# Another order of the sixteen scratch steps of a batch, and other chunks for the value halves

## The chip, the cores and the metric

The kernel runs on one NeuronCore of one Trainium2 chip. The metric is the time of one execution on the device in microseconds (us); smaller is better. TensorE (PE, with PEld for its weight loads) multiplies, ScalarE (ACT) and VectorE (DVE) read its results from PSUM, GpSimd (POOL) and SyncE (SP) do small work and start transfers.

## The reference

One block of cross attention and a mixture of experts, all in float32: 32 batches of 100 tokens of width 128, each batch with its own context of 1444 rows, 16 heads of width 8.

```python
q, k, v = LN(x) @ W_q.T, ctx @ W_k.T, ctx @ W_v.T         # 16 heads of 8
scores  = einsum('bhqd,bhkd->bhqk', q, k) / sqrt(8)
e       = exp(clip(scores, -50, 50)); attn = e / sum(e)
x = x + einsum('bhqk,bhkd->bhqd', attn, v) @ W_o.T
z = LN(x)
comb = top-2 softmax weights of z @ gate_w                # 8 experts
x = x + sum_e comb[e] * (gelu(z @ w1[e]) @ w2[e])
```

## The kernel before

Most of the time goes to the attention, a loop over the 32 batches `b` (function `attend`, once for each engine; the batches 0, 1, 30 and 31 are written out, the others are a hardware loop over pairs). The 1444 keys are 12 tiles of 128 and the 16 heads are 4 groups of 4, so a batch has 48 pairs of a tile and a group; three pairs make a **chunk**, and a batch has 16 chunks, c = 0 to 15. The three matmuls of a chunk (L689) fill one of two PSUM buffers, `scores`. ACT takes the exponential of the chunk (L902) into a ring of 8 chunks in SBUF, `probs`, and DVE clips it there (L1046).

The product with the values has a tile and a half of the heads as its unit, a **half** `h` = 0 to 23. Its four matmuls (L701) each use 17 of the array's columns, one in each of the four column groups, and add to `o_sum`. A matmul in float32 leaves two records, so a half is 8 records, and a row x24 is three halves. `HALF_AT[h]` (L70) is the chunk at which PE does half h; a number of 16 or more means chunk HALF_AT[h] - 16 of the next batch. Half h needs the clipped chunk `LAST_CHUNK[h // 2]`. Chunk c may overwrite its place in the ring once the halves that read chunk c - 8 are done (L901).

Everything else of a batch goes through one further PSUM bank, `scratch`: 16 **scratch steps**, one in each chunk, in the order of the list `STEPS` (L109).

- For the next batch, `PREPARE`: turn 0 to 2 transpose the context (L614) and ACT copies it to `ctxT` (L862); key 0 to 2 project a third of the keys each (L619, 512 columns, the last 420), ACT copies to `k_full` (L866), and DVE splits it in a high and a low part (L960, L962) one chunk later; value 0 to 2 project a third of the values (L630) and DVE copies to `v_both` (L984); query (L624).
- For the batch before, `FINISH`: heads transposes its sums (L662) after DVE took them from `o_sum` (`take_sums`, L1051); queries, project, tokens; gate gives the logits of the experts, with which DVE finds the two best; rank (L682, L683) counts places in the experts' lists.

Since there is one bank, every scratch step waits until the step ahead of it has been copied out: `pe.wait_ge(scratch_emptied, step)` at L645. In a chunk PE does, in this order: the scores of chunk c + 1 (after the exponential of chunk c - 1), the scratch step of chunk c, the halves of chunk c. ACT does the exponential of chunk c, then the copy of the scratch step, if it is ACT's. DVE clips chunk c - 1, then takes its scratch step. The chunks of `take_sums` (L1153), of `pick` (L1167) and of ACT's `second_share` (L906) follow from `HALF_AT` and `STEPS` through `HALF_AT[-1]` and `GATED`. In batch 0 the places of `FINISH` are filled by transposes of normed tokens (L638), and batch 31 has only the steps of `FINISH`. After the attention come the experts, 57 tiles of 128 rows (L797 to L818), which the change leaves alone.

Of the kernel before, what the change touches and what calls it, by code (L numbers as in the profile page):

```python
# [48 lines left out]
def xattn_moe(nc, x, ctx, mask, W_q, W_k, W_v, W_o, gate_w, w1, w2, out):  # L49
# [15 lines left out]
    RING = 8  # L65
    LAST_CHUNK = [(t * GROUPS + GROUPS - 1) // CB for t in range(TILES)]
    HALVES = 2 * TILES
    LAG = 2

    HALF_AT = [4 * (h // 6) + LAG + (2, 2, 2, 4, 4, 4)[h % 6] for h in range(HALVES)]  # L70
    KC = 4
    KSTEPS = TILES // KC

# [27 lines left out]
    PREPARE = [("query", 0)]  # L101
# [4 lines left out]

    FINISH = [("heads", 0), ("queries", 0), ("project", 0), ("tokens", 0), ("gate", 0), ("rank", 0)]

    STEPS = (PREPARE[1:7] + FINISH[:3] + PREPARE[:1] + PREPARE[7:8] + FINISH[3:5] + PREPARE[8:] + FINISH[5:])  # L109
    IN_LAST = [s in FINISH for s in STEPS]  # L110

    ALONE = PREPARE[7:9] + [("first query", n) for n in range(2)] + PREPARE[9:]

    FIRST_STEPS = [s if s in PREPARE else ("norm", QSTEPS - len(FINISH) + FINISH.index(s)) for s in STEPS]
    assert len(STEPS) == CHUNKS and QSTEPS - len(FINISH) == 2
    PROJECTED, GATED = STEPS.index(("project", 0)), STEPS.index(("gate", 0))

    def scratch_step(b, c):

        if isinstance(b, int) and b == B - 1:  # L120
            c = sum(IN_LAST[:c])
        return len(STEPS) * b + len(ALONE) + c

    def planned(b, c):
# [3 lines left out]
        if isinstance(b, int) and b == B - 1 and not IN_LAST[c]:  # L128
            return None, 0
        return STEPS[c]  # L130

# [4 lines left out]
    def later(b, least=1):  # L136

        return not isinstance(b, int) or b >= least
# [7 lines left out]
    with es:  # L146
# [463 lines left out]
        def _(pe):  # L610
# [84 lines left out]
            def weigh_values(p, h):  # L695


                t, s = divmod(h, 2)
                for g in range(GROUPS):
                    c, m = divmod(t * GROUPS + g, CB)  # L700
                    last = nc.tensor.matmul(o_sum[32 * g:32 * g + VW, s * PQ:(s + 1) * PQ],  # L701
                                            v_ones[p][:, t, 2 * g + s, :],
                                            probs[:, c % RING, m, s * PQ:(s + 1) * PQ],
                                            start=(t == 0 and s == 0), stop=(t == TILES - 1),
                                            skip_group_check=True)
                last.then_inc(pv_done, 1)
# [32 lines left out]
            def attend(i, p, b, last_one):  # L739
                for c in range(CHUNKS):  # L740
# [20 lines left out]
                    for h in range(HALVES):  # L761
                        if HALF_AT[h] == c:
                            pe.wait_ge(probs_ready, CHUNKS * b + LAST_CHUNK[h // 2] + 1)
# [5 lines left out]
                            weigh_values(p, h)  # L769
                        elif HALF_AT[h] == c + CHUNKS and later(b):  # L770
                            pe.wait_ge(probs_ready, CHUNKS * (b - 1) + LAST_CHUNK[h // 2] + 1)
# [9 lines left out]
            for h in range(HALVES):  # L781
                if HALF_AT[h] >= CHUNKS:
                    pe.wait_ge(probs_ready, CHUNKS * (B - 1) + LAST_CHUNK[h // 2] + 1)
# [168 lines left out]
        def _(dve):  # L952
# [95 lines left out]
            def take_sums(b):  # L1048

                dve.wait_ge(pv_done, HALVES * (b + 1))  # L1050
                nc.vector.tensor_copy(o_raw[:], o_sum[:, 0:GQ]).then_inc(o_taken, 1)  # L1051
# [99 lines left out]
            def attend(p, b):  # L1151
                for c in range(CHUNKS):
                    if c == HALF_AT[-1] + 1 - CHUNKS and later(b):  # L1153
                        take_sums(b - 1)
# [143 lines left out]
```

## Time and profile before

| what | us |
|---|---|
| median of 3 runs | 1141.67 (1141.52 to 1142.09) |
| the profiled execution | 1142.76 |
| its span, first to last instruction | 1140.8 |
| PE busy | 1042.8 (91%) |
| DVE busy | 757.6 (66%) |
| ACT busy | 741.4 (65%) |
| POOL busy | 258.4 (23%) |

Between 100 and 850 us the granted clock of TensorE is 1.00, that is 2.4 GHz. "Idle before" in a row of the trace is the time that the engine had nothing running before that group, with what released it. Matmuls overlap their neighbours, and their ends are modelled, so the distance between the starts of two rows tells more than their durations.

### The profile page before, as it was taken

The page shows a single profiled execution, that of the slowest core. Times are in us where ns is not written, and L with a number is a line of the kernel's source. Part 1 is how long each engine was busy: PE and PEld are TensorE (multiplying, and loading weights), DVE is VectorE, ACT ScalarE, POOL GpSimd, SP SyncE. Part 2 cuts the span into 40 slices and gives each one's busy share as a digit, 9 for nine tenths or more (in the row PEclk, how much of TensorE's full clock was granted, in tenths as well). Part 3 has the DMA queues.
Part 4 walks back from the last instruction along what each step waited for, and adds up shares of the span by engine and source line. Part 5 has one row for each costly group of instructions (what it writes and reads, how often), then busy time and mean ns, then how long its engine had stood idle before and what let it go on. Part 6 is the DMA issues. An engine that isn't in the chain of part 4 may idle for free.

```text
span 1140.8 us, 30886 instructions
## 1 busy us (share of the span) xinstructions
PE 1042.8 (91%) x10544; PEld 761.5 (67%) x10545; DVE 757.6 (66%) x1956; ACT 741.4 (65%) x960; POOL 258.4 (23%) x324
## 2 busy tenths in 40 slices
PE   4699999999999999999999999999999999399990
PEld 3466666666666666666666666666666667299990
DVE  4557777777777777777777777777777777434443
ACT  2477777777777777777777777777777777244440
POOL 3711111111111111111111111111111112145554
PEclk8699999999999999999999999999999999699995
DMA  6644454444444444445445454444545545022216
GB/s 195 194 151 160 161 170 164 156 158 161 165 164 161 165 156 162 164 169 167 166 166 169 169 169 166 167 167 169 169 169 169 169 140 156 15 68 64 63 48 173
DMA packets 144306, 172.68 MB, mean 151 GB/s; under 512 B 32225, under 2 KB 88549, under 8 KB 144277
## 3 DMA queue, kind: packets, MB, share of 16 engines
q1 hardware_dynamic: 139380, 165.67, 44.0%
q0 software_dynamic: 4896, 6.63, 2.1%
q8 instruction: 17, 0.28, 0.1%
q14 instruction: 13, 0.10, 0.0%
HBM read 36.83 MB, written 22.08 MB: 52 GB/s over the span
## 4 chain that ended last, share of the span: by engine, by line
PE 85%; ACT 3%; DVE 3%; DMA 2%; SPq 2%; issue 2%; POOL 0%; ACTq 0%; POOLq 0%; DVEq 0%
PE o_sum L701 26%; PE scores L689 25%; PE scratch L630 8%; PE scratch L619 7%; PE scratch L614 5%; PE scores L807 5%; PE scores L818 4%; ACT k_full L866 3%; DVE v_both L984 2%; PE scratch L662 2%; DMA x_all<-in_x_dram 1%; SPq L486 1%; PE scratch L667 1%; SPq L405 1%; PE scores L797 1%
## 5 line engine op out<-in xcount | busy, mean ns | idle before, releaser
L902 ACT ACTIVATE probs<-scores 128x1200 f32<-128x1200 f32 x512 | 589.3, 1180 | 88.9 <-PE scores L689 85.9
L689 PE MATMUL scores<-q_stack,k_stack 128*128 128x400 f32 x1536 | 431.5, 395 | 10.4 <-DVE mask_f L1033 10.0
L1046 DVE TENSOR_SCALAR probs<-probs 128x1200 f32<-128x1200 f32 x512 | 387.0, 782 | 49.1 <-ACT probs L902 47.7
L689 PEld LDWEIGHTS scores<-q_stack,k_stack 128*128 128x128 f32 x1536 | 256.0, 190 | 138.6 <-issue 99.0
L701 PE MATMUL o_sum<-probs,v_both 128*17 128x200 f32 x6144 | 309.8, 334 | 0.1
L701 PEld LDWEIGHTS o_sum<-probs,v_both 128*17 128x17 f32 x6144 | 154.8, 97 | 84.1 <-issue 16.7
L573 POOL DMA_INDIRECT expert_rows<-rows,row_atu x64 | 77.5, 1211 | 373.8 <-DMA expert_rows<-fill 314.9
L630 PE MATMUL scratch<-w_turned,ctxT 128*128 128x128 f32 x768 | 108.3, 284 | 8.5 <-DVE v_both L984 7.2
L866 ACT COPY k_full<-scratch 128x512 f32<-128x512 f32 (+1 forms) x93 | 52.2, 561 | 92.9 <-PE scratch L619 91.7
L630 PEld LDWEIGHTS scratch<-w_turned,ctxT 128*128 128x128 f32 x768 | 96.1, 192 | 24.3 <-DVE v_both L984 17.6
L563 POOL TENSOR_SCALAR rstd<-moments 100x1 f32<-100x1 f32 x32 | 37.7, 1177 | 289.5 <-DVE moments L1084 289.5
L619 PE MATMUL scratch<-ctxT,w_turned 128*128 128x512 f32 x186 | 91.0, 571 | 0.0
L984 DVE COPY v_both<-scratch 128x512 f32<-128x512 f32 x93 | 64.1, 689 | 37.8 <-PE scratch L630 35.7
L960 DVE CAST k_hi<-k_full 128x512 fp32r<-128x512 f32 (+1 forms) x93 | 38.7, 416 | 58.4 <-ACT k_full L866 33.4
L597 POOL DMA_INDIRECT expert_outputs<-ctx_nat,tile_home x57 | 57.2, 1004 | 64.6 <-DVE ctx_nat L1248 60.7
L962 DVE TENSOR_TENSOR k_lo<-k_full,k_hi 128x512 fp32r<-128x512 f32 (+1 forms) x93 | 61.5, 661 | 3.2
L818 PE MATMUL scores<-w_sb,k_full 128*128 x456 | 61.6, 279 | 1.3 <-ACT k_full L933 1.3
L807 PE MATMUL scores<-ctxT 128*128 128x128 f32 x456 | 62.4, 281 | 0.0
L933 ACT ACTIVATE k_full<-scores 128x512 f32<-128x512 f32 x57 | 34.1, 598 | 40.2 <-PE scores L807 39.6
L818 PEld LDWEIGHTS scores<-w_sb,k_full 128*128 128x128 f32 x456 | 56.3, 194 | 1.7 <-issue 1.5
L807 PEld LDWEIGHTS scores<-ctxT 128*128 128x128 f32 x456 | 57.1, 197 | 0.3
L862 ACT COPY ctxT<-scratch 128x512 f32<-128x512 f32 (+1 forms) x93 | 52.5, 565 | 4.1 <-PE scratch L614 0.9
(142 smaller groups left out, 753.0 us busy)
## 6 DMA issues: line engine op xcount, KB each, us to landing
k_stack<-k_hi SPq DMA_DIRECT2D x192, 256.0 KB, 2.5
k_stack<-k_lo SPq DMA_DIRECT2D x192, 256.0 KB, 2.6
expert_rows<-fill SPq DMA_DIRECT2D x32, 406.2 KB
xT_and_ctx<-in_ctx_dram SPq DMA_DIRECT2D x16, 704.0 KB
ctx_nat<-in_ctx_dram SPq DMA_DIRECT2D x16, 704.0 KB
q_rep<-q_parts SPq DMA_DIRECT2D x128, 50.0 KB, 1.9
q_stack<-q_rep SPq DMA_DIRECT2D x128, 50.0 KB, 1.9
v_both<-expert_rows SPq DMA_DIRECT2D x57, 65.0 KB, 1.8
```

What stands on the lines that cost most here:

```text
L573: nc.gpsimd.indirect_dma_start(out=expert_rows[0:E * CAP, :], out_offset=bass.IndirectOffsetOnAxis(ap=row_atu[:, k:k + 1], axis=0), in_=ro ...
L619: return nc.tensor.matmul(into[:, 0:KEYS[k]], w_turned[:, WK, :], ctxT[:, KEY_COLS[k]], start=True, stop=True)
L630: last = nc.tensor.matmul(scratch[:, j * P:(j + 1) * P], ctxT[:, t * P:(t + 1) * P], w_turned[:, WV, :], start=True, stop=True)
L689: last = nc.tensor.matmul(scores[:, c % 2, m, 0:GQ], k_stack[p][:, g, t * P:(t + 1) * P], q_stack[p][:, :, g, :], start=True, stop=True)
L701: last = nc.tensor.matmul(o_sum[32 * g:32 * g + VW, s * PQ:(s + 1) * PQ], v_ones[p][:, t, 2 * g + s, :], probs[:, c % RING, m, s * PQ:(s + ...
L807: last = nc.tensor.matmul(scores[:, n % 2, 0, c * P:(c + 1) * P], w1_tile[:, n % 2, c * P:(c + 1) * P], tileT[:, n % 2, :], start=True, st ...
L818: last = nc.tensor.matmul(scores[:, n % 2, 1, 0:D], hiddenT[:, n % 2, c, :], w2_sb[:, bass.ds(expert, 1), c, :].rearrange("f o d -> f (o d)"),
L866: nc.scalar.copy(k_full[:, k, 0:KEYS[k]], scratch[:, 0:KEYS[k]]).then_inc(scratch_emptied, 1)
L902: nc.scalar.activation(probs[:, c % RING, :, :], scores[:, c % 2, :, 0:GQ], ACT.Exp, scale=SCALE).then_inc(exp_ready, 1)
L962: nc.vector.tensor_tensor(k_lo[:, cols], k_full[:, k, 0:KEYS[k]], k_hi[:, cols].bitcast(F32), ALU.subtract).then_inc(k_split, 1)
L984: nc.vector.tensor_copy(v_ones[p][:, k * KC:(k + 1) * KC, :, 0:2 * DH], scratch[:].rearrange("p (t n d) -> p t n d", t=KC, n=PAIRS)).then_ ...
L1046: nc.vector.tensor_scalar(chunk, chunk, LOW, HIGH, ALU.max, ALU.min).then_inc(probs_ready, 1)
```

## The change

It writes out two tables. `STEPS` has the three turns and the three keys as turn, turn, key, turn, key, key (before: turn, key three times), and at the end value 2, gate, value 1, rank (before: gate, value 1, value 2, rank). `HALF_AT` spreads the halves of the chunks 0 to 6: before, the chunks 0, 2, 4 and 6 had three halves each and the odd chunks none; now the chunks 0 to 6 have 1, 1, 2, 1, 1, 1 and 4. Chunk 14 has four instead of three. The last half of a batch moves from chunk 2 of the next batch to chunk 3, and with it `take_sums` from chunk 3 to chunk 4; gate moves from chunk 12 to 13, `pick` from 13 to 14 and `second_share` from 14 to 15. No instruction of arithmetic is added or removed. All line numbers after L108 grow by one.

```diff
-    LAG = 2
-    HALF_AT = [4 * (h // 6) + LAG + (2, 2, 2, 4, 4, 4)[h % 6] for h in range(HALVES)]
+    HALF_AT = [4, 5, 6, 6, 6, 6, 8, 8, 8, 10, 10, 10, 12, 12, 12, 14, 14, 14, 14, 16, 17, 18, 18, 19]
...
-    STEPS = (PREPARE[1:7] + FINISH[:3] + PREPARE[:1] + PREPARE[7:8] + FINISH[3:5] + PREPARE[8:] + FINISH[5:])
+    STEPS = [("turn", 0), ("turn", 1), ("key", 0), ("turn", 2), ("key", 1), ("key", 2),
+             ("heads", 0), ("queries", 0), ("project", 0), ("query", 0), ("value", 0), ("tokens", 0),
+             ("value", 2), ("gate", 0), ("value", 1), ("rank", 0)]
```

PE in the loop's even batches, chunks 2 to 5, before. L614 are turns, L619 keys, L701 halves (x4 is one half), L689 the scores of a chunk:

```order
L614 MATMUL scratch<-ident,ctx_nat1 128x128 x4
L701 MATMUL o_sum<-probs,v_both 17x200 x4
L771 REGISTER_ALU
L701 MATMUL o_sum<-probs,v_both 17x200 x8
L744 REGISTER_ALU
L689 MATMUL scores<-q_stack0,k_stack0 128x400 x3
L645 REGISTER_ALU
L619 MATMUL scratch<-ctxT,w_turned 128x512
L744 REGISTER_ALU
L747 ISA
L689 MATMUL scores<-q_stack0,k_stack0 128x400 x3
L645 REGISTER_ALU
```

The same engine after, from key 0 in chunk 2 to the scores of chunk 4:

```order
L620 MATMUL scratch<-ctxT,w_turned 128x512
L702 MATMUL o_sum<-probs,v_both 17x200 x4
L772 REGISTER_ALU
L702 MATMUL o_sum<-probs,v_both 17x200 x4
L745 REGISTER_ALU
L690 MATMUL scores<-q_stack0,k_stack0 128x400 x3
L646 REGISTER_ALU
L615 MATMUL scratch<-ident,ctx_nat1 128x128 x3
L615 MATMUL scratch<-ident,ctx_nat1 128x36
L702 MATMUL o_sum<-probs,v_both 17x200 x4
L745 REGISTER_ALU
L748 ISA
```

Before, a key had only scores between it and the next step; after, every turn and every key has halves right behind it.

PE in the chunks 12 to 14 before (L675 gate, L630 value):

```order
L675 MATMUL scratch<-gate_sb,zT 100x8
L701 MATMUL o_sum<-probs,v_both 17x200 x12
L689 MATMUL scores<-q_stack0,k_stack0 128x400 x3
L645 REGISTER_ALU
L630 MATMUL scratch<-w_turned,ctxT 128x128 x4
L689 MATMUL scores<-q_stack0,k_stack0 128x400 x3
L645 REGISTER_ALU
L630 MATMUL scratch<-w_turned,ctxT 128x128 x4
L701 MATMUL o_sum<-probs,v_both 17x200 x12
```

And after:

```order
L631 MATMUL scratch<-w_turned,ctxT 128x128 x4
L702 MATMUL o_sum<-probs,v_both 17x200 x12
L690 MATMUL scores<-q_stack0,k_stack0 128x400 x3
L646 REGISTER_ALU
L676 MATMUL scratch<-gate_sb,zT 100x8
L690 MATMUL scores<-q_stack0,k_stack0 128x400 x3
L646 REGISTER_ALU
L631 MATMUL scratch<-w_turned,ctxT 128x128 x4
L702 MATMUL o_sum<-probs,v_both 17x200 x16
```

The gate now stands between the two value steps, and each value step has halves behind it.

## Rows read from the trace of the kernel before

**Rows 1.** The page: span, busy time by engine, and the group of the halves.

```profile
span 1140.8 us, 30886 instructions
...
PE 1042.8 (91%) x10544; PEld 761.5 (67%) x10545; DVE 757.6 (66%) x1956; ACT 741.4 (65%) x960; POOL 258.4 (23%) x324
...
L701 PE MATMUL o_sum<-probs,v_both 128*17 128x200 f32 x6144 | 309.8, 334 | 0.1
```

**Rows 2.** Timeline, PE: value 2 of batch 1 and of batch 30.

```profile
98.85 1.16 PE L630 MATMUL scratch<-w_turned,ctxT 128*128 128x128 f32 x8 [0.23 <-DVE v_both L984]
...
949.61 1.16 PE L630 MATMUL scratch<-w_turned,ctxT 128*128 128x128 f32 x8 [0.23 <-DVE v_both L984]
```

**Rows 3.** Waits of PE, 100 to 900 us: total us, times, longest us.

```profile
PE scratch L630 <- DVE v_both L984: 6.2, 27, 0.2
PE scratch L614 <- ACT k_full L866: 6.0, 29, 0.2
PE scratch L614 <- issue: 5.6, 26, 0.3
```

**Rows 4.** Timeline, PE, chunks 0 to 6 of one batch: start us, us, what.

```profile
513.50 0.60 PE L614 MATMUL scratch<-ident,ctx_nat 128*128 128x128 f32 x4
514.03 1.21 PE L701 MATMUL o_sum<-probs,v_both 128*17 128x200 f32 x24
...
515.83 1.02 PE L619 MATMUL scratch<-ctxT,w_turned 128*128 128x512 f32 x2
...
517.63 0.65 PE L614 MATMUL scratch<-ident,ctx_nat 128*128 128x128 f32 x4 [0.24 <-issue]
...
520.01 1.02 PE L619 MATMUL scratch<-ctxT,w_turned 128*128 128x512 f32 x2
...
521.78 0.73 PE L614 MATMUL scratch<-ident,ctx_nat 128*128 128x128 f32 x4 [0.21 <-ACT k_full L866]
...
524.24 0.87 PE L619 MATMUL scratch<-ctxT,w_turned 128*128 128x420 f32 x2
...
525.77 0.64 PE L662 MATMUL scratch<-ident,o_raw 128*100 128x128 f32 x4
```

**Rows 5.** Timeline, PE, chunks 10 to 14 of the same batch.

```profile
531.06 0.80 PE L689 MATMUL scores<-q_stack,k_stack 128*128 128x400 f32 x3
531.70 1.15 PE L630 MATMUL scratch<-w_turned,ctxT 128*128 128x128 f32 x8
532.77 1.21 PE L701 MATMUL o_sum<-probs,v_both 128*17 128x200 f32 x24
...
534.57 0.25 PE L671 MATMUL scratch<-ident,rows 100*128 100x100 f32 x1
...
535.23 0.27 PE L675 MATMUL scratch<-gate_sb,zT 128*100 128x8 f32 x2
...
537.23 1.05 PE L630 MATMUL scratch<-w_turned,ctxT 128*128 128x128 f32 x8
538.03 0.79 PE L689 MATMUL scores<-q_stack,k_stack 128*128 128x400 f32 x3
539.06 1.16 PE L630 MATMUL scratch<-w_turned,ctxT 128*128 128x128 f32 x8 [0.23 <-DVE v_both L984]
```

**Rows 6.** Timeline, ACT in chunks 1 and 2, DVE in chunk 13 of the same batch.

```profile
516.99 0.59 ACT L866 COPY k_full<-scratch 128x512 f32<-128x512 f32 x1 [1.19 <-PE scratch L619]
517.47 1.18 ACT L902 ACTIVATE probs<-scores 128x1200 f32<-128x1200 f32 x1
518.54 0.59 ACT L862 COPY ctxT<-scratch 128x512 f32<-128x512 f32 x1
...
538.31 0.69 DVE L984 COPY v_both<-scratch 128x512 f32<-128x512 f32 x1 [1.08 <-PE scratch L630]
```

**Rows 7.** Timeline, PE in batch 31: halves, with two chunks of scores between.

```profile
953.53 1.21 PE L701 MATMUL o_sum<-probs,v_both 128*17 128x200 f32 x24
...
955.97 1.21 PE L701 MATMUL o_sum<-probs,v_both 128*17 128x200 f32 x24
```

## Prediction

> **What bounds the kernel now.** I read the page first: PE is busy 91% of the span, DVE and ACT two thirds [rows 1]. Then the timeline of PE over many batches: it repeats itself, and from value 2 of batch 1 to value 2 of batch 30 it takes 949.61 - 98.85 = 850.76 us, 29.34 us for each of the 29 batches [rows 2]. So whatever the change does, it does some thirty times. Then the waits of PE: only three kinds, each about once a batch or less, and the longest is 0.3 us [rows 3]. Their sum over 27 batches is 17.8 us, which makes them look small: 0.66 us a batch. The timeline of one batch shows that they cost more than their idle time says, and where.
>
> I read that timeline from the start of one scratch step to the start of the next, a "block", because the starts don't depend on modelled ends. Blocks with halves behind the step have room for the copy: turn 0 to key 0 takes 515.83 - 513.50 = 2.33 us, turn 1 to key 1 2.38, turn 2 to key 2 2.46 [rows 4]. Blocks with only scores are too short for it: key 0 to turn 1 takes 1.80, key 1 to turn 2 1.77, key 2 to heads 1.53, value 1 to value 2 1.83 [rows 4, 5]. For a value step the part that isn't waiting can be read: the scores start 538.03 - 537.23 = 0.80 us after it, and with no wait the next step starts 0.64 us after the scores (531.06 to 531.70). That is 1.44 us, so this wait costs 1.83 - 1.44 = 0.39 us, not the 0.23 of its row [rows 5]. What it waits for is DVE's copy, which starts 538.31 - 537.23 = 1.08 us after the value step and takes 0.69 [rows 6]. The key steps wait in the same way for ACT's copy, 516.99 - 515.83 = 1.16 us after the step, and 0.59 long [rows 4, 6].
>
> **What halves cost.** The change takes the waits away by putting halves behind each of those steps. The halves aren't new, but a group of them has a fixed part. In a row x24 the four column groups work at once, so it is six rounds of four records; one record takes 0.334 us, and the last round starts 1.21 - 0.334 = 0.88 us after the first, 0.175 us a round [rows 1, 5]. A half is two rounds, 0.35 us. From the start of a group of three halves to the next scratch step are 534.57 - 532.77 = 1.80 us [rows 5]; so with one half it is 1.10, with two 1.45, with four 2.15. Of the 1.80, 1.05 are the six rounds and about 0.6 the scores; the rest, 0.1 to 0.15, and a gap between the scratch step and the group, is what each group adds. Before there are 8 groups a batch, after there are 11.
>
> The distance from a scratch step to the group behind it is 514.03 - 513.50 = 0.53 for a turn and 532.77 - 531.70 = 1.07 for a value step [rows 4, 5]. For a **key** step the trace never shows it, since no key has halves behind it. This is the one number that I must bound. Both groups above start 0.07 to 0.08 us before the modelled end of the step (0.60 and 1.15); by that a key of 512 columns gives 1.02 - 0.07 = 0.95 [rows 4, 5]. The latest is when ACT can read the result, 1.16 [rows 6]. I take 0.98, close to the low end, since for turn and value the group starts so near the modelled end; and 0.15 less, 0.83, for the key of 420 columns, whose row is 0.15 shorter [rows 4].
>
> **Chunks 0 to 6, block by block, after.** Turn 0 with one half to turn 1: 2.33 less two halves, 1.63. Turn 1 to key 0: 1.63. Key 0 with two halves to turn 2: 0.98 + 1.45 = 2.43. Turn 2 with one half to key 1: 2.46 - 0.70 = 1.76. Key 1 to key 2: 0.98 + 1.10 = 2.08. Key 2 to heads: 0.83 + 1.10 = 1.93. Sum 11.46 us; before it was 525.77 - 513.50 = 12.27 [rows 4]. Heads has one half more behind it, + 0.35. Together - 0.46 us a batch.
>
> **Chunks 11 to 14.** Before: tokens to gate 0.66, gate to value 1 2.00, value 1 to value 2 1.83, value 2 with three halves 2.87 as value 0 shows: 7.36 [rows 5]. After: tokens to value 2 0.66 (it waits for the same copy as gate did), value 2 with three halves 2.87, gate with only scores to value 1, value 1 with four halves 3.22. The gate block isn't in the trace: its low end is 0.66, the block of tokens, whose row is as short (0.25 against 0.27), its high end the 1.44 of a value step without a wait; I take 0.75, by the likeness of the rows. Sum 7.50, + 0.14 us a batch.
>
> **Do other waits come?** After turn 0, ACT has 1.10 us from the start of the halves to turn 1, and needs some 0.1 + 0.59 for its copy. ACT itself has an exponential and a copy in every chunk: 0.48 us from a copy to the exponential behind it (516.99 to 517.47) and 1.07 from that to the next copy (518.54), 1.55 in all [rows 6]. The two shortest blocks are 1.63, so ACT just keeps up for two chunks, and the next, 2.43, gives it air. What covers it is thin, 0.08 us a block; if it were gone, turn 1 would start late by the 0.1 or so that is missing, and by the same again at key 0. DVE's move of its copy of `o_sum` by a chunk puts the split of key 0 ahead of it; half 0 waits for that copy, and it has the scores and key 1 in between, about 0.64 + 0.98 us, against a copy of 400 columns, shorter than the 0.69 us of 512 [rows 5, 6]. The gate moves behind a clip on DVE, and picking the two best experts now comes one chunk later, with four halves ahead of rank to hide it. ACT's small exponential of the gate stands behind that of chunk 15 now, and DVE's part of rank waits for it; ACT has no copies in the chunks 12 to 14, so it is ahead there. SP's and POOL's queues keep their order; key 0 is split one chunk later, and its transfers are wanted only in chunk 15. I cost all of these at nothing.
>
> **The sum.** - 0.46 + 0.14 = - 0.32 us a batch, thirty batches: - 9.6 us. Batch 0 loses the wait between its value steps (- 0.39) and does one half more (+ 0.35): nothing. Batch 31 has the three groups more without the waits: a group of three halves with two chunks of scores takes 955.97 - 953.53 = 2.44, less 1.05 for the rounds and 2 x 0.6 for the scores leaves 0.2 a group, + 0.6 us [rows 7]. The half fewer after the last chunk I credit at nothing, since that stretch ends with the last clip. Total - 9.0 us. Against the profiled execution, 1142.8 (its span of 1140.8 [rows 1] and 2.0 around it), that is 1133.8; the median of the runs lies 1.1 lower, 1141.67, so **1132.7 us**, 0.8% faster.
>
> **The rivals.** *Better*: the group starts behind a key as soon as its columns have passed. The low end is the 0.10 us that a turn has above its four matmuls; the keys then save another 0.1 each, and the restarts after a wait go too (turn 1 to key 1 is 0.05 longer than turn 0 to key 0, turn 2 to key 2 0.13 [rows 4]): 0.3 to 0.45 us a batch more, 1119 to 1124 us.
>
> *No change*: the waits go, but ACT or DVE gives some back, 0.1 at each of turn 1, key 0 and value 1. Then - 0.32 becomes 0: 1141 to 1143 us. For it speaks the thin cover of ACT in the chunks 0 and 1; against it, that each engine has a third of its time free [rows 1].
>
> *Slower*: the array can't go over from a wide matmul to the halves before the wide one has wholly left it. A key then gives 1.16 us to its group instead of 0.98 [rows 4, 6], + 0.18 for three keys, + 0.54 a batch: - 0.32 becomes + 0.22, 30 x 0.22 = 6.6, 1148 us. It decides from 1.09 us for a key: 0.98 + 0.32 / 3. For it speaks that there are three groups more in every batch whatever happens to the waits; against it, that turn and value show the group starting before their modelled ends [rows 4, 5]. The Trainium skill, TensorEngine Tiling (Array Packing), section Key Properties, has a rule that speaks against this change: going from one tiling mode to another drains TensorE. The trace agrees in kind: 1.07 us from a value step to its halves, 0.80 from one to its scores [rows 5]. The page has no price for it, so by the page alone the three groups more would be a loss of unknown size.
>
> **Chances.** The forecast, 1128 to 1138: 0.56. Better: 0.14. No change and its neighbourhood up to 1144: 0.18. Slower beyond: 0.12. For the range, 1124 to 1145 leaves about 0.1 on each side. A measurement of this kernel can tell some 0.2%, 2.3 us, from no change; faster than 1139.4 gets 0.76, between that and 1144.0 gets 0.12, slower 0.12.
>
> **What would show it.** In the trace of after: no idle time of PE before L615, L631 and L663 in the loop (right), or a new row of waits on ACT before L615 (the second rival). A distance from L620 of 512 columns to the L702 behind it of about 0.98; 1.09 or more gives the third rival. The block of one half after a turn 1.63, the gate block 0.75. The period of a batch 29.0 us. The prediction is wrong if the groups cost more in a mix of short ones than in threes, which no row of before shows.

## Result and profile after

The changed kernel takes 1127.31 us in the median of 4 runs (1125.29 to 1128.25), against 1141.88 (1141.52 to 1143.66) before: ratio 0.9863, 95% interval 0.9849 to 0.9878, or 14.6 us less. The profiled execution took 1127.23 us.

The page of after answers to [rows 1]: the span, the busy times, the group of the halves.

```profile
span 1125.1 us, 30886 instructions
...
PE 1047.4 (93%) x10544; PEld 752.2 (67%) x10545; DVE 761.0 (68%) x1956; ACT 744.2 (66%) x960; POOL 274.7 (24%) x324
...
L702 PE MATMUL o_sum<-probs,v_both 128*17 128x200 f32 x6144 | 328.1, 335 | 0.5 <-DVE probs L1047 0.5
```

The three kinds of waits of [rows 3] have no successor: between 100 and 900 us the list of PE's waits is empty. PE's busy time grew by 4.6 us while the span fell by 15.7: what the waits gave back was in part spent on more and smaller groups of halves. They are busy 328.1 us where they were 309.8, with no half added: a row of one half lasts 0.53 us, a row of three 1.21 and not 3 x 0.53, so splitting a group adds about 0.2 us to the busy time. The starts of the rank step in batch 1 and in batch 30 give the period of a batch, (935.88 - 101.56) / 29 = 28.77 us, where it was 29.34 [rows 2].

```profile
101.56 0.27 PE L683 MATMUL scratch<-chosen,before 100*100 100x8 f32 x2
...
935.88 0.26 PE L683 MATMUL scratch<-chosen,before 100*100 100x8 f32 x2
...
957.54 0.31 PE L683 MATMUL scratch<-chosen,before 100*100 100x8 f32 x2
```

The same steps in the kernel before: rank of the batches 1, 30 and 31.

```profile
101.73 0.26 PE L682 MATMUL scratch<-chosen,before 100*100 100x8 f32 x2
...
952.50 0.26 PE L682 MATMUL scratch<-chosen,before 100*100 100x8 f32 x2
...
973.09 0.34 PE L682 MATMUL scratch<-chosen,before 100*100 100x8 f32 x2
```

These six rows hold the whole account of the two spans. Up to the rank step of batch 1 after is 0.17 us earlier; the next 29 batches take 834.32 instead of 850.77 us, 16.45 less; batch 31 takes 957.54 - 935.88 = 21.66 instead of 20.59, 1.07 more; what follows takes 0.15 less (1125.1 - 957.54 = 167.56 against 1140.8 - 973.09 = 167.71). Sum: - 15.7 us.

Timeline of PE after, chunks 0 to 6 of one batch, answering to [rows 4] (L615 turns, L620 keys, L702 halves, L663 heads):

```profile
505.30 0.60 PE L615 MATMUL scratch<-ident,ctx_nat 128*128 128x128 f32 x4
505.83 0.53 PE L702 MATMUL o_sum<-probs,v_both 128*17 128x200 f32 x8
...
506.95 0.60 PE L615 MATMUL scratch<-ident,ctx_nat 128*128 128x128 f32 x4
...
508.60 1.02 PE L620 MATMUL scratch<-ctxT,w_turned 128*128 128x512 f32 x2
509.55 0.87 PE L702 MATMUL o_sum<-probs,v_both 128*17 128x200 f32 x16
510.36 0.82 PE L690 MATMUL scores<-q_stack,k_stack 128*128 128x400 f32 x3
511.02 0.67 PE L615 MATMUL scratch<-ident,ctx_nat 128*128 128x128 f32 x4
...
512.73 1.02 PE L620 MATMUL scratch<-ctxT,w_turned 128*128 128x512 f32 x2
...
514.80 0.87 PE L620 MATMUL scratch<-ctxT,w_turned 128*128 128x420 f32 x2
...
516.73 0.60 PE L663 MATMUL scratch<-ident,o_raw 128*100 128x128 f32 x4
...
519.39 0.25 PE L666 MATMUL scratch<-ident,attn 100*128 100x100 f32 x1
```

No row has an idle time. The halves start 509.55 - 508.60 = 0.95 us after the key. From turn 0 to heads are 11.43 us, and heads takes 2.66 to the next step. The chunks 11 to 15, answering to [rows 5] (L672 tokens, L631 values, L676 gate, L683 rank):

```profile
525.81 0.25 PE L672 MATMUL scratch<-ident,rows 100*128 100x100 f32 x1
...
526.47 1.09 PE L631 MATMUL scratch<-w_turned,ctxT 128*128 128x128 f32 x8
527.48 1.21 PE L702 MATMUL o_sum<-probs,v_both 128*17 128x200 f32 x24
...
529.27 0.26 PE L676 MATMUL scratch<-gate_sb,zT 128*100 128x8 f32 x2
...
530.02 1.05 PE L631 MATMUL scratch<-w_turned,ctxT 128*128 128x128 f32 x8
531.01 1.55 PE L702 MATMUL o_sum<-probs,v_both 128*17 128x200 f32 x32
...
533.14 0.26 PE L683 MATMUL scratch<-chosen,before 100*100 100x8 f32 x2
```

Value 2 with three halves takes 2.80 to the next step, the gate 0.75, value 1 with four halves 3.12.

### The profile page after: what moved, and what is told of

The parts are those of the page before. It is cut to its first block, busy times and chain, and to the rows that moved or that the text cites. A ratio compares the mean times of both kernels' runs of the same rounds, so it can differ in the third digit from the quotient of the medians.

```text
span 1125.1 us, 30886 instructions
## 1 busy us (share of the span) xinstructions
PE 1047.4 (93%) x10544; PEld 752.2 (67%) x10545; DVE 761.0 (68%) x1956; ACT 744.2 (66%) x960; POOL 274.7 (24%) x324
## 4 chain that ended last, share of the span: by engine, by line
PE 91%; DMA 3%; SPq 2%; DVE 2%; issue 1%; ACT 0%; POOL 0%; POOLq 0%; DVEq 0%
PE scores L690 32%; PE o_sum L702 27%; PE scratch L631 8%; PE scratch L620 7%; PE scores L808 5%; PE scores L819 4%; PE scratch L615 4%; DMA x_all<-in_x_dram 1%; SPq L487 1%; PE scratch L663 1%; PE scratch L668 1%; SPq L406 1%; PE scores L798 1%; PE scratch L625 1%; PE scratch L684 1%
## 5 line engine op out<-in xcount | busy, mean ns | idle before, releaser
L690 PE MATMUL scores<-q_stack,k_stack 128*128 128x400 f32 x1536 | 406.3, 380 | 10.4 <-DVE mask_f L1034 9.9
L690 PEld LDWEIGHTS scores<-q_stack,k_stack 128*128 128x128 f32 x1536 | 248.6, 189 | 129.3 <-issue 73.3
L702 PE MATMUL o_sum<-probs,v_both 128*17 128x200 f32 x6144 | 328.1, 335 | 0.5 <-DVE probs L1047 0.5
L702 PEld LDWEIGHTS o_sum<-probs,v_both 128*17 128x17 f32 x6144 | 145.0, 97 | 144.2 <-issue 58.0
L631 PE MATMUL scratch<-w_turned,ctxT 128*128 128x128 f32 x768 | 106.2, 282 | 1.3 <-ACT v_both L892 0.7
L631 PEld LDWEIGHTS scratch<-w_turned,ctxT 128*128 128x128 f32 x768 | 96.1, 192 | 10.2 <-ACT q_full L874 4.7
L620 PE MATMUL scratch<-ctxT,w_turned 128*128 128x512 f32 x186 | 90.2, 566 | 0.0
```

The costliest lines, as they stand in the source:

```text
L620: return nc.tensor.matmul(into[:, 0:KEYS[k]], w_turned[:, WK, :], ctxT[:, KEY_COLS[k]], start=True, stop=True)
L631: last = nc.tensor.matmul(scratch[:, j * P:(j + 1) * P], ctxT[:, t * P:(t + 1) * P], w_turned[:, WV, :], start=True, stop=True)
L690: last = nc.tensor.matmul(scores[:, c % 2, m, 0:GQ], k_stack[p][:, g, t * P:(t + 1) * P], q_stack[p][:, :, g, :], start=True, stop=True)
```

## Experiments

Two theories were set against each other. **Prices**: each wait behind a long copy has its price, and each group of halves has one; the change swaps the one for the other, and the sum of the blocks tells the time. **Evenness**: the gain comes from chunks of more even length. All kernels below do the whole computation.

| kernel | ratio to before | 95% interval | period of a batch, us |
|---|---|---|---|
| before | 1 | | 29.34 |
| changed | 0.9863 | 0.9849 to 0.9878 | 28.77 |
| values' order alone | 0.9897 | 0.9880 to 0.9915 | 28.97 |
| halves alone | 0.9960 | 0.9946 to 0.9974 | 29.15 |
| all steps, halves of before | 0.9916 | 0.9900 to 0.9933 | 29.06 |
| changed, three groups more | 1.0047 | 1.0028 to 1.0066 | 29.47 |
| changed, beside the next three | 0.9865 | 0.9848 to 0.9881 | 28.77 |
| changed, turns 0 and 2 bare | 0.9870 | 0.9854 to 0.9887 | 28.77 |
| new order, ten groups | 0.9932 | 0.9915 to 0.9948 | 28.93 |
| new order, project covered | 0.9917 | 0.9901 to 0.9934 | 28.91 |

Each ratio is to the kernel before, run beside that kernel on the same chip. The periods are read as above, rank of batch 1 to rank of batch 30, divided by 29. They have far less spread than the times: the two profiles of the changed kernel have spans of 1125.1 and 1121.7 us and the same period.

**The values' order alone.**

```diff
-             ("heads", 0), ..., ("tokens", 0), ("gate", 0), ("value", 1), ("value", 2), ("rank", 0)]
+             ("heads", 0), ..., ("tokens", 0), ("value", 2), ("gate", 0), ("value", 1), ("rank", 0)]
```

> Only the last four scratch steps are new (value 2, gate, value 1, rank); turns, keys and the halves are as before. Price theory: a wait behind a value step costs 0.39 us, and the four blocks from tokens to rank go from 7.37 us to about 7.0 with the halves of before, so 0.37 us a batch, 11 us in all, ratio to before 0.990. The waits of PE on ACT's copies of the keys stay, 0.2 to 0.3 us each. Rival, evenness theory (the gain comes from chunks of more even length, not from single waits): nothing or under 3 us, since the chunks are as uneven as before.

Measured 0.9897 and 0.37 us a batch less, as the prices had it; evenness, with under 3 us, fell. The waits of PE on the copies of the keys are still there (first the list of PE's waits, of which this is the largest, then the timeline of PE, key 0 and turn 1):

```profile
PE scratch L615 <- ACT k_full L867: 6.5, 31, 0.3
...
509.12 1.02 PE L620 MATMUL scratch<-ctxT,w_turned 128*128 128x512 f32 x2
509.58 1.11 PE L690 MATMUL scores<-q_stack,k_stack 128*128 128x400 f32 x3
510.91 0.66 PE L615 MATMUL scratch<-ident,ctx_nat 128*128 128x128 f32 x4 [0.22 <-issue]
```

So two thirds of the gain, 0.37 of 0.57 us, come from putting the gate between two value steps, in a stretch where no group of halves was added.

**The halves alone.**

```diff
-    HALF_AT = [4 * (h // 6) + LAG + (2, 2, 2, 4, 4, 4)[h % 6] for h in range(HALVES)]
+    HALF_AT = [4, 5, 6, 6, 6, 6, 8, 8, 8, 10, 10, 10, 12, 12, 12, 14, 14, 14, 14, 16, 17, 18, 18, 19]
```

> Only the halves are spread as in the change; the order of the scratch steps is the old one. Price theory: the waits behind the keys go, three groups of halves at 0.28 us each come, the wait between the two value steps stays: 0.23 us a batch less than before, 7 us, ratio 0.994. Rival, evenness theory: most of the 15 us of the change, ratio near 0.988.

Measured 0.9960 and 0.19 us a batch less; evenness, with 0.988, fell here too. The waits behind the keys are gone, and the one between the value steps is the only one left in the list of PE's waits:

```profile
PE scratch L631 <- DVE v_both L985: 6.3, 27, 0.2
```

0.37 and 0.19 add up to 0.56; the whole change has 0.57. What is left for the third part of the change, the order of turns and keys, is 0.01. No kernel leaves out that part alone, but the timeline of this one confirms it. From turn 0 to heads, with the old order and the halves spread, are 522.60 - 511.18 = 11.42 us, and 11.43 in the changed kernel:

```profile
511.18 0.60 PE L615 MATMUL scratch<-ident,ctx_nat 128*128 128x128 f32 x4
...
522.60 0.60 PE L663 MATMUL scratch<-ident,o_raw 128*100 128x128 f32 x4
```

With the halves spread, that order is worth nothing.

**All steps, halves of before.** The new `STEPS` with the old `HALF_AT`.

> Only the order of the scratch steps is new; the halves are where they were, in eight groups of three. Bare of halves are now turn 1, turn 2 and key 2. Price theory: a turn without halves is followed by the next step after about 1.25 us (copy seen 0.6 after its start, 0.59 long) where 1.04 is the least, so it costs 0.2 to 0.25, less than the 0.28 of a group; sum of the blocks from turn 0 to rank 21.2 us against 22.0 before and 21.4 in the changed kernel: 24 us less than before, 7 less than the changed kernel, ratio 0.979. Rival, evenness theory: slower than the changed kernel, 0.99 at best, since its chunks are as uneven as before.

Measured 0.9916, 29.06 us. It is slower than the changed kernel, and by 0.09 us a batch slower than with the values' order alone; 24 us less than before had been expected, 9.0 were measured. Two reasons stand in the timeline, PE first, for turn 1 and key 0 in a batch of even and one of odd number:

```profile
512.17 0.60 PE L615 MATMUL scratch<-ident,ctx_nat 128*128 128x128 f32 x4
512.52 0.79 PE L690 MATMUL scores<-q_stack,k_stack 128*128 128x400 f32 x3
513.89 1.13 PE L620 MATMUL scratch<-ctxT,w_turned 128*128 128x512 f32 x2 [0.57 <-issue]
...
541.45 0.60 PE L615 MATMUL scratch<-ident,xT_and_ctx 128*128 128x128 f32 x4
...
542.72 1.13 PE L620 MATMUL scratch<-ctxT,w_turned 128*128 128x512 f32 x2
```

ACT in the same two places:

```profile
513.25 0.59 ACT L863 COPY ctxT<-scratch 128x512 f32<-128x512 f32 x1 [1.11 <-PE scratch L615]
...
542.09 0.59 ACT L863 COPY ctxT<-scratch 128x512 f32<-128x512 f32 x1 [0.66 <-PE scratch L615]
```

In the odd batch a turn without halves takes 1.27 us to the next step, as expected. In the even one it takes 1.72, since ACT starts its copy 1.08 us after the turn instead of 0.64, though it had nothing else to do. The list of PE's waits has this 13 times:

```profile
PE scratch L620 <- issue: 6.9, 12, 0.6
PE scratch L620 <- ACT ctxT L863: 1.3, 1, 1.3
```

The timeline says where: in batch 4, the longest (1.33 us idle), and in the batches 6, 8, to 28 (0.53 to 0.60). These are the 13 passes of the loop's body that follow a jump back. In batch 2, the first pass of the same code, the same turn takes 1.27 us (105.00 to 106.27), and so it does in batch 30, which is written out (919.13 to 920.40). So the delay goes with the jump back and not with the code. The changed kernel doesn't show it: there the exponential on ACT runs up to this copy, which starts 0.64 us after turn 1 in an even batch too. And a key behind a turn without halves needs 0.10 us more (a row of 1.13 instead of 1.02) before its halves start, which the expectation had left out.

Evenness had this kernel right, but it had the two before wrong.

**Three groups more.**

```diff
-    HALF_AT = [4, 5, 6, 6, 6, 6, 8, 8, 8, 10, 10, 10, 12, 12, 12, 14, 14, 14, 14, 16, 17, 18, 18, 19]
+    HALF_AT = [4, 5, 6, 6, 6, 6, 8, 8, 9, 10, 10, 11, 12, 12, 13, 14, 14, 14, 14, 16, 17, 18, 18, 19]
```

> The changed kernel with one half of each of the chunks 8, 10 and 12 moved to the chunk behind it (9, 11 and 13), where no copy is late: three groups of halves more, no wait taken away. Price theory: 3 x 0.28 = 0.84 us a batch more than the changed kernel, 25 us, so ratio to before about 1.008. Rival (a group costs next to nothing, what the change bought was the waits): equal to the changed kernel, 0.986.

Measured 1.0047, 0.70 us a batch more than the changed kernel: 0.23 us for each group, not 0. With no wait in sight, moving three halves by one chunk makes the kernel slower than the one before. Block by block, the group behind the query costs 0.31, the one behind tokens 0.31 and the one behind the gate 0.22, 0.28 in the mean as expected. The sum is smaller because the first of them bought something. Timeline of PE, query to tokens:

```profile
503.54 0.36 PE L625 MATMUL scratch<-xT_and_ctx,w_turned 128*128 x2
503.83 0.53 PE L702 MATMUL o_sum<-probs,v_both 128*17 128x200 f32 x8
...
504.95 1.05 PE L631 MATMUL scratch<-w_turned,ctxT 128*128 128x128 f32 x8
505.93 0.87 PE L702 MATMUL o_sum<-probs,v_both 128*17 128x200 f32 x16
```

Value 0 reaches its halves after 0.98 us here, and after 1.07 in the kernel before [rows 5]. Before, it stood right behind the query with only scores between, and its first weight load waited for ACT's copy of the query. That is in the list of all waits of the kernel before (100 to 900 us), and not in the list of this one:

```profile
PEld scratch L630 <- ACT q_full L873: 4.5, 27, 0.2
```

It is a wait of the weight load, which PE's own list does not have, because the scores were still running. The change leaves it: the changed kernel has it 28 times, 4.7 us in all.

**Turns bare.** From the changed kernel; nine groups. To make room in the chunks 4 and 5, chunk 6 has two halves instead of four, and the last half of a batch is back in chunk 2.

```diff
+    HALF_AT = [4, 4, 5, 5, 6, 6, 8, 8, 8, 10, 10, 10, 12, 12, 12, 14, 14, 14, 14, 17, 17, 18, 18, 18]
```

> The changed kernel's order of steps, but turn 0 and turn 2 have no halves behind them; their halves join the groups of the chunks 1, 2, 4 and 5, so there are nine groups instead of eleven. Price theory, with the prices of the first four runs: a turn without halves takes 1.27 us to the next step and that step 0.1 more for its restart, against 1.65 with one half, of which 0.33 is the half: no gain and no loss to 0.1 us a batch, so the ratio is that of the changed kernel within 0.003, possibly up to 0.008 more if ACT's copy is late after the loop's jump, as the turn's copy in the kernel with the steps alone was in every second batch (0.45 us). Rival, group theory (only the number of groups counts): 2 x 0.28 us a batch less, 17 us, ratio 0.971.

Measured 0.9870 beside 0.9865 for the changed kernel on the same chip, the same period to 0.01 us. Two groups fewer gain nothing, for a turn without halves costs what a group costs. The late copy that the expectation allowed for didn't come. The number of groups alone decides nothing: the rival's 0.971 fell. Turn 0 and turn 1 of this kernel:

```profile
505.99 0.60 PE L615 MATMUL scratch<-ident,ctx_nat 128*128 128x128 f32 x4
506.56 0.82 PE L690 MATMUL scores<-q_stack,k_stack 128*128 128x400 f32 x3
507.26 0.65 PE L615 MATMUL scratch<-ident,ctx_nat 128*128 128x128 f32 x4
```

1.27 us from turn to turn, with no idle time in any row: the scores start 0.57 us after the turn instead of the 0.35 of the kernel with all steps, so a wait can hide in where the scores stand. The exponential that they need ended 0.05 us earlier, at 506.51 (ACT, 505.34 + 1.17).

**A new order with ten groups, and with project covered.**

```diff
+    STEPS = [("turn", 0), ("query", 0), ("turn", 1), ("key", 0), ("turn", 2), ("heads", 0),
+             ("queries", 0), ("key", 1), ("project", 0), ("key", 2), ("value", 0), ("tokens", 0),
+             ("value", 1), ("gate", 0), ("value", 2), ("rank", 0)]
+    HALF_AT = [3, 3, 4, 4, 5, 5, 7, 7, 9, 9, 9, 10, 12, 12, 12, 12, 14, 14, 14, 16, 16, 18, 18, 18]
```

The second has `HALF_AT[8] = 8`.

> Another order of the steps: turn 0, query, turn 1, key 0, turn 2, heads, queries, key 1, project, key 2, value 0, tokens, value 1, gate, value 2, rank. No step with a long copy stands ahead of another without halves between, and the halves are in ten groups (chunks 0, 2, 3, 4, 5, 7, 9, 10, 12, 14) instead of eleven. Project has none behind it. Price theory: one group less, - 0.28; value 0 no longer stands right behind the query, whose copy made its weight load late, - 0.08; DVE's step of project (about 0.35 long, seen 0.56 after the step's start) leaves a wait of 0.1 to 0.2 before key 2: together - 0.15 to - 0.25 us a batch, 5 to 8 us less than the changed kernel, ratio 0.979 to 0.982. Rival: ACT can't keep up where two of its copies of turns and keys follow small steps, and gives it back: 0.986 or more.

> The order of the kernel with ten groups, but one half stands behind project, taken from chunk 9: eleven groups again. Price theory: one group more, + 0.28, the wait behind project gone, - 0.1 to - 0.2: 0.1 to 0.2 us a batch, 3 to 6 us, slower than the kernel with ten groups; still 1 to 3 us faster than the changed kernel, for value 0. Rival, evenness theory: faster than ten groups, since the chunks are more even.

Measured 0.9932 and 0.9917, both slower than the changed kernel; their intervals overlap, so which of the two is faster stays open. The rival of the first expectation was right. The second expectation, 3 to 6 us slower than ten groups, was wrong: the medians are 1.6 us apart the other way, the periods 0.02. The block of project with one half behind it is 1.42 us (521.40 to 522.82 in that kernel), and without it 1.09, shorter by the half alone: the wait costs as much there as the group. In the kernel with ten groups, PE around the query, turn 1 behind it, then around project:

```profile
510.05 0.36 PE L625 MATMUL scratch<-xT_and_ctx,w_turned 128*128 x2
510.41 0.82 PE L690 MATMUL scores<-q_stack,k_stack 128*128 128x400 f32 x3
511.07 0.60 PE L615 MATMUL scratch<-ident,ctx_nat 128*128 128x128 f32 x4
...
522.95 0.38 PE L668 MATMUL scratch<-w_turned,attnT 128*100 128x128 f32 x2
523.38 0.82 PE L690 MATMUL scores<-q_stack,k_stack 128*128 128x400 f32 x3
524.04 0.87 PE L620 MATMUL scratch<-ctxT,w_turned 128*128 128x420 f32 x2
```

ACT ahead of them:

```profile
509.18 1.18 ACT L903 ACTIVATE probs<-scores 128x1200 f32<-128x1200 f32 x1
...
522.15 2.25 ACT L903 ACTIVATE probs<-scores 128x1200 f32<-128x1200 f32 x2
```

The scores behind the query start 0.36 us after it, 0.05 after the exponential that they need has ended (509.18 + 1.18 = 510.36). ACT was late with it because a turn's copy stood ahead. The block is 1.02 us where the query took 0.78 before the change and 0.77 after. Behind project the scores start after 0.43 and the block is 1.09; the exponential they need is the first of the two from 522.15, and it stands behind the copy of key 1. A small step right behind a step with a long copy of ACT makes the chunk too short for ACT. The change's own order has its small steps without halves behind steps whose copies are short or are DVE's.

## Why the prediction came out as it did

The direction, the mechanism and the range were right; the gain, 14.6 us in the medians, was larger than the 9.0 that the sum gave. The measured 1127.31 lies just below the forecast's own 1128 to 1138, between it and the better rival's 1119 to 1124, and what was missing in the sum was in part what that rival named.

- **Waits.** All of them went, at each of the places named. The wait between the value steps was priced at 0.39; the kernel with the values' order alone saves 0.37. That is a net figure: with the wait goes the restart behind it (0.07), and three halves cost some 0.09 more behind a value step than behind the gate.
- **Key to halves**, the number that had to be bounded: 0.95 us, where 0.98 was taken and 0.95 was the low end by the two other kinds of step. The end of 1.16 rested on the start of ACT's copy, and that is not the start of the next group: behind a key ACT starts at 1.14 to 1.16 in both kernels, while the halves start at 0.95. The third rival fell with it, and so did the half of the better rival that had the keys 0.1 shorter still.
- **Chunks 0 to 6**: 11.46 forecast, 11.43 measured.
- **The gate block**: 0.75 forecast, 0.75 measured. The bounds were 0.66 and 1.44; the likeness to the block of tokens chose the right end, the exact hit was luck.
- **The term that was mis-sized** is the block of a step with three or four halves, taken from value 0 and from heads. Value 0 is the one value step whose weights come late, behind the query, so its 1.07 us to the halves and its 2.87 us block were no fair sample: value 2 has 1.01 and 2.80, value 1 0.99. Heads was read from a batch in which it had waited, and a step that waited takes some 0.05 to 0.1 us more: 2.66, not 2.73. And a half measures 0.335 us, not 0.35: from the start of a group to the scores behind it are 0.47 us for one half, 0.81 for two, 1.48 for four (505.83 to 506.30 and so on). For value 1 with four halves that makes 3.12 instead of 3.22. Together 0.07 + 0.07 + 0.10 = 0.24 us a batch, 7 us in all. Against the two profiles, 15.7 us apart, the miss is 6.7 us, since batch 31 took 0.5 back; in the medians it is 5.6. The prediction had these restarts, but only in the better rival, not in the sum.
- **Batch 31** gave back 1.07 us, not 0.6. Read block by block, the three groups cost 0.92, that is 0.31 each and not 0.2. The other 0.15 lies between tokens and rank: picking the two best experts ends at 957.40 (DVE, 957.23 + 0.17), and the last rank step starts at 957.54, 0.15 us after its halves would have let it. The prediction had this at nothing, with four halves to hide it; with three halves, as in the kernel with the values' order alone, the same step stands idle for 0.42 us.
- **Other waits**: ACT's thin cover in the chunks 0 and 1 held, 1.65 us a block. That it was thin was right, as the kernel with ten groups shows.
- The Trainium skill, TensorEngine Tiling (Array Packing), section Key Properties, says that a change of tiling mode drains TensorE. The traces agree in kind, though none shows the drain itself. The prediction's pair for it was not a fair one: of the 1.07 us from a value step to its halves 0.09 were the late weights, so it is 0.98 to 1.01 against the 0.80 to the scores. What a group costs here is 0.22 to 0.31 us. It doesn't turn the sign, because a key's wait costs a little more than that.

What stays open: why ACT starts its copy 0.4 us late, and only behind the loop's jump back; no kernel without the loop was tried.

## To carry to other kernels

Read a repeating schedule as distances between the starts of successive steps, and price every wait and every interleaved group from them; the idle time in a row of the trace is only a part of a wait, and a wait of the weight load or a late start of the filler work shows in no idle time at all. Before a filler is put behind a step to hide a copy, compare its own fixed price with the wait: here 0.22 to 0.31 us against some 0.4 behind a value step, an estimated 0.3 or a little over behind a key (three of these waits less three groups leave 0.19 us a batch in the kernel with the halves alone), and behind a turn no more than the group itself. And take the sample of a block from one that neither waited nor stands behind a late copy. An order of steps that needs no filler (a cheap step between two with long copies) is worth more than filler (0.37 against 0.19 us a batch here), as long as the engine that copies can keep the pace.

## What the runs showed that had not been expected

- The fixed price of a group, 0.22 to 0.31 us, shows as no idle time. Behind a turn it can be read: the halves start 0.53 us after it where scores alone start after 0.35, and the scores follow the start of one half after 0.47, where a half takes 0.335. That makes 0.31.
- ACT started a copy 1.08 us after the turn in the passes behind the loop's jump back (1.84 in the first of them), and 0.64 in the first pass of the same code.
- Two profiles of the same kernel had the same period, 28.77 us, and spans of 1125.1 and 1121.7 us; 2.8 us of that lie behind the last rank step of the loop over the batches (167.6 and 164.8). The period can tell kernels apart that the whole time doesn't.
